# A four-layer attention and experts model on one core: the softmax division's transfers issued by ScalarE, the output bias added by GpSimd, and loads and projection chunks moved within the beginnings of two expert stages

## The chip, the core and the metric

The kernel runs on one core of one Trainium2 chip. A core has four compute engines that take their instructions in order and meet by semaphores: TensorE (PE; its weight loads are listed as PEld), VectorE (DVE), ScalarE (ACT) and GpSimd (POOL), and SyncE (SP), which here only issues DMA transfers. ACT and POOL issue DMA transfers too, as instructions in their own streams. The metric is the time of one execution on the device in microseconds, lower is better.

## The reference

Four layers work on x of shape (4, 512, 256) in float32, each a gated cross attention over a context of 1601 positions and a gated feed-forward stage. The attention of layers 0, 1 and 2 has 16 heads of depth 16:

```python
q = (layernorm(x) @ Wq + bq)   # layer 1 also rotates q and k (rope)
k, v = ctx @ Wk + bk, ctx @ Wv + bv
attn = softmax(q k^T / scale)              # (4, 16, 512, 1601)
x = x + tanh(g) * ((attn @ v) @ Wo + bo)
```

The feed-forward stage of layer 0 is one linear layer with quantised input and ternary weights. Those of layers 1 and 2 are mixtures of 8 experts, of which each row of x takes the one with the highest gate (relu in layer 1, gelu and a capacity in layer 2):

```python
idx = argmax(softmax(x @ gate))            # one expert per row
y[r] = act(x[r] @ w1[idx] + b1[idx]) @ w2[idx] + b2[idx]
```

Layer 3 has an attention with one head of depth 256, and a feed-forward stage that takes two of 8 experts per row.

## The kernel before

**Attention (layers 0, 1 and 2).** The four batches are worked off one after the other, and in each the 16 heads in NG = 4 groups of HG = 4 heads. A group is 13 key tiles of 128 positions times 4 heads, 52 jobs. A job is one matmul of scores s (L1320, on PE) and one exponential e_t (L1412, on ACT). After each key tile PE multiplies e_t with the values of the four heads into pv (L1334). Beside these jobs PE computes maxima of scores for a group some way ahead (m, L1298), which DVE reduces (L1181). `Plan` writes the order of all this down once as a list of units; each engine goes through the whole list and carries out its share, so the place of a unit in the list is its place in each engine's stream. `attend(g, b, *work)` lays the 52 jobs of a group out and spreads other generators of units evenly between them.

**The division by the softmax sums.** When a group's 13 tiles are done, ACT copies pv (outputs and sums of four heads, 128x512) into z (L1419). The rest belongs to the next group: `normalise` gives, one step after the other, the units sum, rec, spread, a step without a unit, and norm.

- sum: SP waits for z and issues rc<-z (L915: the sums, as 128x16) and four ot<-z (L918: the outputs).
- rec: DVE waits for these five transfers (one semaphore, "moved", counts all) and takes the reciprocal of rc (L1204).
- spread: SP waits for the reciprocal, stores rc to DRAM (L927 sums<-rc), waits until that has landed, and loads it back, once for each of 64 partitions (L930 ot<-sums).
- norm: after every second group DVE multiplies the outputs of 8 heads with these reciprocals (L1207).

Then, once for each batch, PE projects with Wo, and DVE adds gate times the product to x and adds the scaled output bias bob (L1213, one per row tile, 16 per layer). The transfers of the division stand in SP's queue among loads and stores of keys and values; between two batches of layer 1 they stand behind the stores of split queries (qready, L94), which wait for GpSimd.

**Other work on ACT.** In a middle group ACT also takes over the values of a finished group for the next batch (v<-vn, L1406, unit take), and in layer 2 it issues beside each take a transfer that clears a part of a table in DRAM (xregion<-zero, L1429, ten times).

**The experts (layers 1 and 2).** The stage normalises x, transposes it (L150), computes the gates (L2382), from them each row's place (L2391, L2392), and scatters the rows to the places by indirect DMA (xs<-xn). SP loads the tiles of rows back (xt<-xs, L2160), and PE runs the two layers of the experts. Into the beginning of layer 1's stage is woven the projection of keys and values of the next attention in chunks of 512 positions (`Prepared`: L322 keys, L330 values on PE, L349 and following on ACT, splits into parts by the engines that its last argument names, stores by SP). In layer 2's stage SP loads the experts' second weights (L2146, eight matrices of 1 MB) and three pieces of the context for the stage after (kT, L1508), and a piece is let out only when a buffer is free of the piece ahead of it.

Of the kernel before, what the change touches and what calls it, by code (L numbers as in the profile page):

```python
# [12 lines left out]
B, T, D, S2 = 4, 512, 256, 1601  # L13
# [422 lines left out]
NORM_STEPS = 5  # L436

MOVES = 1 + HG + 2
# [26 lines left out]
class Plan:  # L465
# [16 lines left out]
    def add(self, kind, **f):  # L482
# [15 lines left out]
        if kind in ("pv", "turn", "sum", "rec", "spread", "norm", "take", "peak"):  # L498
            u.n = self.next(kind)
# [193 lines left out]
def head_attention(kn, w, gate, scale, rope, mask, ready, setup, late):  # L693
# [4 lines left out]
    with ctx:  # L698
# [72 lines left out]
        for name, n in (("s_full", plan.count["s"]), ("s_free", plan.count["s"]), ("m_full", plan.count["m"]),  # L771
# [3 lines left out]
                        ("filled", 2), ("b_scaled", 1), ("bv_made", 1), ("x_done", 1)):  # L775
# [3 lines left out]
        sig("moved", DMA).close(MOVES * NG * B)  # L779
        ends = ["x_done", "s_free", "z_full", "r_full", "td", "moved"]  # L780
# [27 lines left out]
def head_sp(kn, a):  # L808
# [39 lines left out]
    for at, u in enumerate(plan.units):  # L848
# [50 lines left out]


def head_sum_sp(kn, a, u):

    sp, z_full, m_full, moved = kn.nc.sync, kn.sema("z_full"), kn.sema("m_full"), kn.sema("moved", DMA)
    sp.wait_ge(z_full.sem, z_full.at(u.n + 1))
    if u.n:
        sp.wait_ge(moved.sem, moved.at(MOVES * u.n))
    if u.b:
        outs = [x for x in a.plan.units if x.kind == "out" and x.b == u.b - 1]
        sp.wait_ge(m_full.sem, m_full.at(outs[-1].m + 1))
    elif a.p and u.g == 0:  # L910

        for f in range(a.p.RING):
            kept = kn.sema(f"p_k{f}", DMA)
            sp.wait_ge(kept.sem, kept.at(a.p.stores[f]))
    sp.dma_start(a.rc[:], a.z[HD::P // HG, :]).then_inc(moved.sem, DMA)  # L915
    for j in range(HG):
        to, of = HG * HD * (u.g % 2) + HD * j, P // HG * j
        sp.dma_start(a.op[to:to + HD, u.g // 2, :], a.z[of:of + HD, :]).then_inc(moved.sem, DMA)  # L918


def head_spread_sp(kn, a, u):

    sp, r_full, moved = kn.nc.sync, kn.sema("r_full"), kn.sema("moved", DMA)
    sums = kn.dram["sums"]
    sp.wait_ge(r_full.sem, r_full.at(u.n + 1))
    sp.wait_ge(moved.sem, moved.at(MOVES * u.n + 1 + HG))
# [2158 lines left out]
```

## Time and profile before

| what | value |
|---|---|
| time before, median of 3 runs | 3891.18 us (3888.99 to 3891.73) |
| the profiled execution's own time | 3877.86 us |
| span of the profile | 3876.7 us |
| mean granted clock of PE | 0.938 |
| busy share of the span: PE, DVE, ACT, POOL | 88%, 56%, 52%, 17% |
| chain that ended last: PE, DVE, DMA, ACT, SP's queue | 65%, 14%, 7%, 3%, 2% |

The span is that of the instructions in one execution recorded by the hardware profiler; the profiled execution's own time is 1.2 us longer, and both lie 13 us under the median of the runs without a profile. A busy share is an average over stages of different kinds; the rows below come from the stages that the change touches. The attention of layer 0 lies at 0 to 857 us of the span, that of layer 1 at 1042 to 1838, layer 1's experts at 1838 to 2147, layer 2's attention at 2147 to 2920, and its experts from there to about 3150.

### The profile page before, as it was taken

The numbers are of one execution on the slowest core, as the hardware profiler recorded it, in microseconds if no ns is written. First come the engines' busy times: TensorE is split into PE (matmuls) and PEld (weight loads), VectorE is DVE, ScalarE is ACT, GpSimd is POOL, SyncE is SP. The second block draws the span as 40 slices with busy tenths as digits, with TensorE's granted clock in tenths as the row PEclk, the third lists the DMA queues.
The fourth block names the chain that finished last, engine by engine and source line by source line (L and its number), as shares of the span: only waits on it lengthen the run. The fifth ranks groups of instructions, "written<-read, shape, count | busy, mean of one in ns | idle before, by whom it ended". The sixth has DMA issues, their size and how long they took to land.

```text
span 3876.7 us, 52367 instructions
## 1 busy us (share of the span) xinstructions
PE 3409.0 (88%) x18396; PEld 1775.9 (46%) x18396; DVE 2180.8 (56%) x3567; ACT 2033.8 (52%) x4490; POOL 653.1 (17%) x700
## 2 busy tenths in 40 slices
PE   5899999978588899997799699889986979987997
PEld 3333333325332233332588333223325956677996
DVE  6767676736757677873401477768843033265334
ACT  2566666653236566766333167567771322244664
POOL 2111111001125331000302131210002020022331
PEclk8999999999779999999899699999997989998998
DMA  8132323105664343310865555654207521042555
GB/s 191 43 102 63 102 63 102 24 26 185 165 181 118 94 106 74 61 24 14 276 219 176 170 157 119 173 115 100 78 10 277 177 89 56 13 139 88 179 179 177
DMA packets 314686, 456.02 MB, mean 118 GB/s; under 512 B 66315, under 2 KB 234195, under 8 KB 312251
## 3 DMA queue, kind: packets, MB, share of 16 engines
q1 hardware_dynamic: 243382, 292.39, 27.5%
q0 software_dynamic: 29568, 104.65, 7.9%
q10 hardware_dynamic: 41477, 55.63, 5.1%
q8 instruction: 150, 2.46, 0.3%
q14 instruction: 109, 0.89, 0.1%
HBM read 292.46 MB, written 153.91 MB: 115 GB/s over the span
## 4 chain that ended last, share of the span: by engine, by line
PE 65%; DVE 14%; DMA 7%; issue 5%; POOL 4%; ACT 3%; SPq 2%; ACTq 0%; POOLq 0%; DVEq 0%
PE pv L1334 14%; PE m L1298 10%; DVE mxp L1181 10%; PE s L1320 9%; PE h L2794 5%; PE y L2802 5%; PE h L2368 4%; PE y L2377 3%; PE y L1779 2%; PE s L1759 2%; PE s L1265 2%; PE m L1342 1%; ACT e_t L1412 1%; PE s L1282 1%; DMA ot<-sums 1%
## 5 line engine op out<-in xcount | busy, mean ns | idle before, releaser
L1181 DVE TENSOR_REDUCE mxp<-m 128x1 f32<-128x802 f32 x1536 | 1447.7, 985 | 522.4 <-PE m L1298 519.8
L1412 ACT ACTIVATE e_t<-s 128x512 f32<-128x512 f32 (+1 forms) x2496 | 1338.9, 600 | 569.3 <-PE s L1320 568.6
L1298 PE MATMUL m<-kaug,qaug 97*128 97x401 bf16 x3072 | 811.4, 347 | 111.1 <-DVE mxp L1181 60.9
L1320 PE MATMUL s<-qaug,kaug 100*128 100x512 bf16 (+1 forms) x2496 | 857.4, 386 | 22.7 <-ACT e_t L1412 18.4
L1334 PE MATMUL pv<-e_t,v 128*32 128x512 f32 (+1 forms) x4992 | 670.2, 609 | 0.2
L1320 PEld LDWEIGHTS s<-qaug,kaug 100*128 100x128 bf16 (+1 forms) x2496 | 228.1, 99 | 715.6 <-ACT e_t L1412 496.6
L1298 PEld LDWEIGHTS m<-kaug,qaug 97*128 97x128 bf16 x3072 | 273.8, 100 | 521.3 <-DVE mxp L1181 280.5
L127 POOL TENSOR_TENSOR rstd<-rstd,mhalf 128x16 f32<-128x16 f32 (+2 forms) x9 | 24.2, 2687 | 1203.2 <-DVE rstd L120 1203.2
L2864 ACT ACTIVATE ez<-h,b 128x128 f32<-128x128 f32 x440 | 119.8, 387 | 160.0 <-PE h L2794 160.0
L1334 PEld LDWEIGHTS pv<-e_t,v 128*32 128x32 f32 (+1 forms) x4992 | 98.6, 108 | 214.6 <-ACT e_t L1412 155.5
L2255 DVE SCALAR_TENSOR_TENSOR y<-y,b 128x256 f32<-128x256 f32 x39 | 16.6, 424 | 309.5 <-PE y L2377 309.5
L2666 DVE TENSOR_SCALAR ez<-ez 128x1024 f32<-128x1024 f32 x55 | 38.1, 694 | 225.9 <-ACT z L2864 225.9
L1071 POOL TENSOR_TENSOR kr<-kf,ks 128x512 f32<-128x512 f32 (+1 forms) x78 | 77.9, 999 | 497.3 <-ACT ks L1384 493.1
L2451 ACT ACTIVATE hT<-h,b 128x128 f32<-128x128 f32 x312 | 84.7, 382 | 127.6 <-PE h L2368 127.5
L2368 PE MATMUL h<-xtT,w 128*128 128x128 f32 x1248 | 149.8, 280 | 0.4 <-ACT xtT L2468 0.3
L2802 PE MATMUL y<-w,hT 128*128 x624 | 143.0, 383 | 5.7 <-DVE hT L2667 5.7
L2368 PEld LDWEIGHTS h<-xtT,w 128*128 128x128 f32 x1248 | 146.5, 196 | 1.1 <-ACT xtT L2468 1.0
L2794 PE MATMUL h<-xtT,w 128*128 128x128 f32 x1248 | 147.0, 276 | 0.0
L2794 PEld LDWEIGHTS h<-xtT,w 128*128 128x128 f32 x1248 | 143.9, 193 | 0.1
L2377 PE MATMUL y<-w,hT 128*128 x624 | 140.9, 379 | 0.0
L2802 PEld LDWEIGHTS y<-w,hT 128*128 128x128 f32 x624 | 116.7, 192 | 20.9 <-issue 6.3
L2864 ACT ACTIVATE z<-h,b 128x128 f32<-128x128 f32 x440 | 122.5, 453 | 0.0
(370 smaller groups left out, 3560.6 us busy)
## 6 DMA issues: line engine op xcount, KB each, us to landing
w<-in_L_w POOLq DMA_DIRECT2D x78, 1024.0 KB, 5.2
w<-in_L_w SPq DMA_DIRECT2D x24, 1024.0 KB, 12.8
xregion<-zero ACTq DMA_DIRECT2D x10, 2056.0 KB, 12.5
kaug<-kparts SPq DMA_DIRECT2D x16, 1200.8 KB
kaug<-kready SPq DMA_DIRECT2D x32, 600.4 KB
kaug<-kready SPq DMA_DIRECT2D x16, 1200.8 KB
vn<-values SPq DMA_DIRECT2D x8, 1536.0 KB
values<-p_vb ACTq DMA_DIRECT2D x21, 512.0 KB, 4.5
```

Of the source, the lines that this page charges most:

```text
L1071: kn.settle(eng, own, eng.tensor_tensor(rest, src, parts[0], ALU.subtract))
L1181: dve.tensor_reduce(a.mxp[:, u.g % 2, half, n:n + 1], a.m_slot[u.m % 2][:].rearrange("p (a n) -> p a n", a=2)[:, :, 0:PIECE + 1], AX.XY, A ...
L1298: m = pe.matmul(slot[:, 512 * k:512 * k + PIECE + 1], a.qaug[0:R_MAX, u.g, j, P * qc:P * qc + P], a.kaug[0:R_MAX, u.g, j, k0:k0 + PIECE + ...
L1320: pe.matmul(slot[0:KW[u.k], :], a.kaug[0:R_ALL, u.g, u.j, P * u.k:P * u.k + KW[u.k]], a.qaug[0:R_ALL, u.g, u.j, :], start=True, stop=True) ...
L1334: m = pe.matmul(a.pv[32 * j:32 * j + 32, :], a.v[0:KW[u.k], u.k, u.g, VW * j:VW * j + 32], a.e_t[0:KW[u.k], u.n % 2, j, :], start=u.k == 0 ...
L1412: act.activation(a.e_t[0:KW[u.k], e % 2, u.j, :], a.s_slot[u.s % 3][0:KW[u.k], :], ACT.Exp).then_inc(s_free.sem, 1)
L2368: m = pe.matmul(a.h_slot[i % 2][:, P * f:P * f + P], a.w1[:, w1_at, c, P * f:P * f + P], xT(c), start=c == 0, stop=c == DC - 1)
L2377: m = pe.matmul(a.y_slot[i % 2][:, 0:D], a.hT[:, i % 2, f, :], w2(f), start=f == 0, stop=f == FC - 1)
L2451: t = act.activation(a.hT[:, p, f, :], slot[:, P * f:P * f + P], func, bias=bias(f))
L2794: m = pe.matmul(a.h_slot[i % 2][:, P * f:P * f + P], w1[:, c, P * f:P * f + P], xT(c), start=c == 0, stop=c == DC - 1)
L2802: m = pe.matmul(a.y_slot[i % 2][:, 0:D], a.hT[:, i % 2, f, :], w2(f), start=f == 0, stop=f == FC - 1)
L2864: t = act.activation(to[:, p, P * f:P * f + P], slot[:, P * f:P * f + P], func, bias=bias(f))
```

## The change

It has four parts.

1. **The division's transfers are issued by ACT.** `head_sum_sp` and `head_spread_sp` go from SP, and `head_sum_act`, `head_low_act` and `head_spread_act` come to ACT, in the same places of the list of units. A new unit, low, holds the store sums<-rc, which stood in spread before; `normalise` has six steps instead of five. The count is split: "moved" counts the four ot<-z, "summed" the other three transfers, and the reciprocal waits for rc<-z alone.
2. **The output bias is added by GpSimd.** At the unit bias, early in the stage, GpSimd adds bob to x in four instructions per layer (128x1024 each); the 16 additions per layer on DVE go, and the wait for the multiply-add ahead of each.
3. **Layer 1's experts.** The prepared projection's first part of two chunks becomes two parts of one chunk each, both split by GpSimd.
4. **Layer 2's experts.** All eight loads of second weights stand ahead of the second and third piece of the context.

```diff
@@ Plan
-NORM_STEPS = 5
+NORM_STEPS = 6
     def normalise(self, g, b):
-        for kind in ("sum", "rec", "spread"):
+        for kind in ("sum", "rec", "low", "spread"):
             self.add(kind, b=b, g=g)
             yield
...
@@ SP
-        elif u.kind == "sum":
-            head_sum_sp(kn, a, u)
-        elif u.kind == "spread":
-            head_spread_sp(kn, a, u)
...
@@ POOL
+        elif u.kind == "bias":
+            pool.wait_ge(b_made.sem, b_made.at(3))
+            for b in range(B):
+                xb = kn.x[:, TT * b:TT * b + TT, :]
+                pool.tensor_tensor(xb, xb, a.bob[:].rearrange("p (t n) -> p t n", t=1).to_broadcast([P, TT, D]),
+                                   ALU.add).then_inc(biased.sem, 1)
...
@@ DVE
         elif u.kind == "rec":
-            dve.wait_ge(moved.sem, moved.at(MOVES * u.n + 1 + HG))
+            dve.wait_ge(summed.sem, summed.at(3 * u.n + 1))
             dve.reciprocal(a.rc[:], a.rc[:]).then_inc(r_full.sem, 1)
         elif u.kind == "norm":
-            dve.wait_ge(moved.sem, moved.at(MOVES * 2 * (u.n + 1)))
+            dve.wait_ge(moved.sem, moved.at(HG * 2 * (u.n + 1)))
+            dve.wait_ge(summed.sem, summed.at(3 * 2 * (u.n + 1)))
...
         elif u.kind == "out":
+            if u.k == 0:
+                dve.wait_ge(biased.sem, biased.at(u.b + 1))
             dve.wait_ge(m_full.sem, m_full.at(u.m + 1))
             dve.scalar_tensor_tensor(xt, a.m_slot[u.m % 2][:, 0:D], a.gate, xt, ALU.mult, ALU.add).then_inc(m_free.sem, 1)
-            dve.wait_ge(m_free.sem, m_free.at(u.m + 1))
-            i = dve.tensor_tensor(xt, xt, a.bob[:], ALU.add)
...
@@ ACT
+        elif u.kind == "sum":
+            head_sum_act(kn, a, u)
+        elif u.kind == "low":
+            head_low_act(kn, a, u)
+        elif u.kind == "spread":
+            head_spread_act(kn, a, u)
...
+def head_sum_act(kn, a, u):
...
+    act.wait_ge(z_full.sem, z_full.at(u.n + 1))
+    if u.n:
+        act.wait_ge(moved.sem, moved.at(HG * u.n))
+        act.wait_ge(summed.sem, summed.at(3 * u.n))
...
+    act.dma_start(a.rc[:], a.z[HD::P // HG, :]).then_inc(summed.sem, DMA)
+    for j in range(HG):
+        to, of = HG * HD * (u.g % 2) + HD * j, P // HG * j
+        act.dma_start(a.op[to:to + HD, u.g // 2, :], a.z[of:of + HD, :]).then_inc(moved.sem, DMA)
...
+def head_low_act(kn, a, u):
...
+    act.wait_ge(r_full.sem, r_full.at(u.n + 1))
+    act.dma_start(sums.rearrange("j (a c) -> (j a) c", a=P // HG), a.rc[:]).then_inc(summed.sem, DMA)
...
+def head_spread_act(kn, a, u):
...
+    act.wait_ge(summed.sem, summed.at(3 * u.n + 2))
+    lo = HG * HD * (u.g % 2)
+    act.dma_start(a.rs[lo:lo + HG * HD, u.g // 2, :],
+                 kn.dram["sums"].rearrange("j (a n) -> j a n", a=1).to_broadcast([HG, HD, T])).then_inc(summed.sem, DMA)
...
@@ experts
-                           ((2, ("pool",)), (1, ("dve",)), (5, ("dve",)), (4, ("dve",))))
+                           ((1, ("pool",)), (1, ("pool",)), (6, ("dve",)), (4, ("dve",))))
...
-        if a.f and e in (0, NE // 2):
-            fold_context_sp(kn, a.f, 3 if e == 0 else 0)
+        if a.f and e == 0:
+            fold_context_sp(kn, a.f, 3)
         sp.dma_start(a.w2[:, e, :, :], w["w2"][e].rearrange("(f p) n -> p f n", p=P)).then_inc(ld_w.sem, DMA)
...
     if a.f:
-        fold_context_sp(kn, a.f, 1)
+        for b in range(2):
+            fold_context_sp(kn, a.f, b)
```

ACT's stream in a middle group of layer 2, before the change. COPY z is the end of the group ahead, and each ACTIVATE is one exponential; s_178 to s_180 are the three buffers of scores:

```order
L1419 COPY z<-pv 128x512
...
L1412 ACTIVATE e_t<-s_179 128x512
L1429 DMA xregion<-zero 2048x1x257
L1406 COPY v<-vn 128x13x4x16
L1412 ACTIVATE e_t<-s_180 128x512
```

The same group after the change:

```order
L1391 COPY z<-pv 128x512
...
L1410 DMA rc<-z 128x1x16
L1413 DMA ot<-z 16x512 x4
...
L1439 DMA xregion<-zero 2048x1x257
L1371 COPY v<-vn 128x13x4x16
L1377 ACTIVATE e_t<-s_180 128x512
...
L1421 DMA sums<-rc 128x16
...
L1428 DMA ot<-sums 64x1x512
```

Seven transfers now stand between ACT's exponentials: five together some five exponentials after z, the store five exponentials behind the clear and the take, and the load back eight further on.

PE's stream at the beginning of layer 1's experts, before the change. L322 and L330 with p_ctx are the prepared projection of 512 positions, L2382 the gates, and L2391 and L2392 the rows' places; ahead of the rows of L150 stands one more run of chunks:

```order
L150 MATMUL y_147<-ident,hT 128x128 x2
L2382 MATMUL b_142<-gw,xnT 128x8 x32
L322 MATMUL h_144<-p_ctx,p_wk 128x512 x4
L330 MATMUL h_145<-p_wv,p_ctx 128x256 x4
L330 MATMUL h_144<-p_wv,p_ctx 128x256 x4
L2391 MATMUL b_142<-oh,tri 128x128
L2392 MATMUL b_143<-oh,ones 128x128
L322 MATMUL h_145<-p_ctx,p_wk 128x65 x4
L330 MATMUL h_144<-p_wv,p_ctx 65x256 x2
```

The same place after the change:

```order
L150 MATMUL y_147<-ident,hT 128x128 x2
L2394 MATMUL b_142<-gw,xnT 128x8 x32
L322 MATMUL h_145<-p_ctx,p_wk 128x512 x4
L330 MATMUL h_144<-p_wv,p_ctx 128x256 x4
L330 MATMUL h_145<-p_wv,p_ctx 128x256 x4
L2403 MATMUL b_142<-oh,tri 128x128
L2404 MATMUL b_143<-oh,ones 128x128
L322 MATMUL h_144<-p_ctx,p_wk 128x512 x4
L330 MATMUL h_145<-p_wv,p_ctx 128x256 x4
L330 MATMUL h_144<-p_wv,p_ctx 128x256 x4
L322 MATMUL h_145<-p_ctx,p_wk 128x65 x4
L330 MATMUL h_144<-p_wv,p_ctx 65x256 x2
```

Of two chunks that stood ahead of the transposes of L150 one has gone behind the places' matmuls.

SP's queue at the beginning of layer 2's experts, before the change:

```order
L1508 DMA kT<-in_ctxT 128x2x1601
L2146 DMA w_202<-in_L_w 128x8x256 x4
L1508 DMA kT<-in_ctxT 128x2x1601
L2146 DMA w_202<-in_L_w 128x8x256 x4
L1508 DMA kT<-in_ctxT 128x2x1601
L2160 DMA xt<-xs 128x256 x5
```

The same place after the change:

```order
L1518 DMA kT<-in_ctxT 128x2x1601
L2156 DMA w_202<-in_L_w 128x8x256 x8
L1518 DMA kT<-in_ctxT 128x2x1601 x2
L2171 DMA xt<-xs 128x256 x5
```

The second piece of the context now stands behind the last four matrices instead of ahead of them.

## Rows read from the trace of the kernel before

**Rows 1.** windows: busy us of PE, PEld, DVE, ACT, POOL; clock, DMA share, GB/s

```profile
1600.00:1700.00 100.00, 97.05 (x559) 31.43 (x557) 80.79 (x107) 72.32 (x135) 0.00 (x0) 1.00 0.21 41
```

**Rows 2.** DVE's reciprocals, layer 2: start, us, engine, line, op, tiles, idle before

```profile
2511.56 0.24 DVE L1204 RECIPROCAL rc<-rc 128x16 f32<-128x16 f32 x1
...
2550.61 0.24 DVE L1204 RECIPROCAL rc<-rc 128x16 f32<-128x16 f32 x1
...
2807.96 0.24 DVE L1204 RECIPROCAL rc<-rc 128x16 f32<-128x16 f32 x1
...
2846.94 0.24 DVE L1204 RECIPROCAL rc<-rc 128x16 f32<-128x16 f32 x1
```

**Rows 3.** waits: who for whom, us in total, times, longest

```profile
DVE rc L1204 <- DMA ot<-z: 145.5, 11, 29.9
DVE ot L1207 <- DMA ot<-sums: 52.9, 7, 13.8
```

**Rows 4.** the end of layer 2's attention, ACT and DVE in order of time

```profile
2903.08 0.58 ACT L1419 COPY z<-pv 128x512 f32<-128x512 f32 x1 [1.19 <-PE pv L1334]
...
2908.17 0.25 DVE L1204 RECIPROCAL rc<-rc 128x16 f32<-128x16 f32 x1 [29.87 <-DMA ot<-z]
...
2920.15 0.42 DVE L1213 TENSOR_TENSOR x<-x,bob 128x256 f32<-128x256 f32 x1
```

**Rows 5.** DVE's waits ahead of three norms, in order of time

```profile
1350.41 1.00 DVE L1207 TENSOR_TENSOR ot<-ot 128x512 f32<-128x512 f32 x1 [13.80 <-DMA ot<-sums]
...
2432.66 1.37 DVE L1207 TENSOR_TENSOR ot<-ot 128x512 f32<-128x512 f32 x1 [12.59 <-DMA ot<-sums]
...
2608.26 0.69 DVE L1207 TENSOR_TENSOR ot<-ot 128x512 f32<-128x512 f32 x1 [9.48 <-DMA ot<-sums]
```

**Rows 6.** SP's DMA issues in order of time, layer 1, between two batches

```profile
1340.32 1.58 SPq L94 DMA_DIRECT2D qready<-ks  x3
...
1343.87 0.52 SPq L927 DMA_DIRECT2D sums<-rc  x1
1346.78 0.57 SPq L930 DMA_DIRECT2D ot<-sums  x1
```

**Rows 7.** SP's issues of one group's store and load, layer 2, beside a clear

```profile
2511.83 0.34 SPq L927 DMA_DIRECT2D sums<-rc  x1
2520.23 0.59 SPq L930 DMA_DIRECT2D ot<-sums  x1
```

**Rows 8.** SP's DMA issues of one group's sums and parts

```profile
1632.70 0.61 SPq L915 DMA_DIRECT2D rc<-z  x1
1633.35 2.46 SPq L918 DMA_DIRECT2D ot<-z  x4
```

**Rows 9.** ACT in order of time around that clear and a take

```profile
2510.88 0.56 ACTq L1429 DMA_DIRECT2D xregion<-zero  x1
2511.47 0.90 ACT L1406 COPY v<-vn 128x832 f32<-128x832 f32 x1
```

**Rows 10.** DMA issues by kind: KB each, median us from issue to landing

```profile
xregion<-zero ACTq DMA_DIRECT2D x10, 2056.0 KB, 12.5
...
xt<-xs SPq DMA_DIRECT2D x39, 128.0 KB, 3.1
```

**Rows 11.** the beginning of layer 1's experts, PE and ACT in order of time

```profile
1853.62 3.60 PE L322 MATMUL h<-p_ctx,p_wk 128*128 128x512 f32 x8
1857.05 3.62 PE L330 MATMUL h<-p_wv,p_ctx 128*128 128x256 f32 x16
...
1904.32 0.69 ACT L349 ACTIVATE p_kf<-h,p_bk 128x512 f32<-128x512 f32 x1 [12.96 <-DMA kready<-p_ks]
```

**Rows 12.** layer 2's experts' beginning: SP's issues, then the critical chain

```profile
2962.89 15.33 SPq L2146 DMA_DIRECT2D w<-in_L_w  x4
...
2991.30 5.97 DMA xs<-xn,to_u
...
2997.29 7.07 DMA xt<-xs
```

More of the change, by code:

```diff
@@ L497, in add @@
             u.m = self.next("m")
-        if kind in ("pv", "turn", "sum", "rec", "spread", "norm", "take", "peak"):
+        if kind in ("pv", "turn", "sum", "rec", "low", "spread", "norm", "take", "peak"):
             u.n = self.next(kind)
@@ L778, in head_attention @@
             sig(name, DMA).close(n)
-        sig("moved", DMA).close(MOVES * NG * B)
-        ends = ["x_done", "s_free", "z_full", "r_full", "td", "moved"]
+        sig("moved", DMA).close(HG * NG * B)
+        sig("summed", DMA).close(3 * NG * B)
+        ends = ["m_free", "s_free", "z_full", "r_full", "td", "moved", "summed"]
         if not ready:
@@ L898, in head_sp @@
                              a.tm[16 * k:16 * k + 16, :]).then_inc(td.sem, DMA)
[L901 to L926, printed above, removed]
-    sp.dma_start(sums.rearrange("j (a c) -> (j a) c", a=P // HG), a.rc[:]).then_inc(moved.sem, DMA)
-    sp.wait_ge(moved.sem, moved.at(MOVES * u.n + 2 + HG))
-    lo = HG * HD * (u.g % 2)
-    sp.dma_start(a.rs[lo:lo + HG * HD, u.g // 2, :],
-                 sums.rearrange("j (a n) -> j a n", a=1).to_broadcast([HG, HD, T])).then_inc(moved.sem, DMA)
 def head_ready_sp(kn, a, n_of):
@@ L1139, in head_dve @@
     turns = units("turn")
-    ot_full, moved = kn.sema("ot_full"), kn.sema("moved", DMA)
+    ot_full, moved, summed, biased = kn.sema("ot_full"), kn.sema("moved", DMA), kn.sema("summed", DMA), kn.sema("biased")
     ld_q = kn.sema("ld_q", DMA)
@@ L1348, in head_act @@
     s_full, s_free, m_free, pv_done = (kn.sema(n) for n in ("s_full", "s_free", "m_free", "pv_done"))
-    z_full, v_taken, b_scaled, filled = (kn.sema(n) for n in ("z_full", "v_taken", "b_scaled", "filled"))
+    z_full, v_taken, b_made, filled = (kn.sema(n) for n in ("z_full", "v_taken", "b_made", "filled"))
     ld_k = kn.sema("ld_k", DMA)
     rope = a.rope is not None
-    moved = kn.sema("moved", DMA)
+    moved, summed = kn.sema("moved", DMA), kn.sema("summed", DMA)
     if not a.ready:
@@ L1417, in head_act @@
             if n:
-                act.wait_ge(moved.sem, moved.at(MOVES * (n - 1) + 1 + HG))
+                act.wait_ge(moved.sem, moved.at(HG * n))
+                act.wait_ge(summed.sem, summed.at(3 * (n - 1) + 1))
             act.copy(a.z[:], a.pv[:]).then_inc(z_full.sem, 1)
+def head_sum_act(kn, a, u):
+    act, z_full, m_full = kn.nc.scalar, kn.sema("z_full"), kn.sema("m_full")
+    moved, summed = kn.sema("moved", DMA), kn.sema("summed", DMA)
+    act.wait_ge(z_full.sem, z_full.at(u.n + 1))
+    if u.n:
+        act.wait_ge(moved.sem, moved.at(HG * u.n))
+        act.wait_ge(summed.sem, summed.at(3 * u.n))
+    if u.b:
+        outs = [x for x in a.plan.units if x.kind == "out" and x.b == u.b - 1]
+        act.wait_ge(m_full.sem, m_full.at(outs[-1].m + 1))
+    elif a.p and u.g == 0:
+        for f in range(a.p.RING):
+            kept = kn.sema(f"p_k{f}", DMA)
+            act.wait_ge(kept.sem, kept.at(a.p.stores[f]))
+    act.dma_start(a.rc[:], a.z[HD::P // HG, :]).then_inc(summed.sem, DMA)
[3 more added lines that the diff above has]
+def head_low_act(kn, a, u):
+    act, r_full, summed = kn.nc.scalar, kn.sema("r_full"), kn.sema("summed", DMA)
+    sums = kn.dram["sums"]
+    act.wait_ge(r_full.sem, r_full.at(u.n + 1))
+    act.dma_start(sums.rearrange("j (a c) -> (j a) c", a=P // HG), a.rc[:]).then_inc(summed.sem, DMA)
+def head_spread_act(kn, a, u):
+    act, summed = kn.nc.scalar, kn.sema("summed", DMA)
+    act.wait_ge(summed.sem, summed.at(3 * u.n + 2))
+    lo = HG * HD * (u.g % 2)
+    act.dma_start(a.rs[lo:lo + HG * HD, u.g // 2, :],
+                 kn.dram["sums"].rearrange("j (a n) -> j a n", a=1).to_broadcast([HG, HD, T])).then_inc(summed.sem, DMA)
 def clear_act(kn, a, nth):
@@ L2196, in experts_pool @@
     if a.p and a.p.in_parts:
-        prepare_split(kn, a.p, a.p.keys_of(0), pool, "pool")
+        for part in range(2):
+            prepare_split(kn, a.p, a.p.keys_of(part), pool, "pool")
     pool.wait_ge(zeroed.sem, zeroed.at(XTILES))
@@ L2922, in setup_dve @@
     dve, cst = kn.nc.vector, kn.cst
-    ident, ready = kn.sema("ident", DMA), kn.sema("set")
+    ident, ready = kn.sema("tables", DMA), kn.sema("set")
     dve.memset(cst["ones"][:], 1.0)
```

35 lines of the change are left out of this document (14 added, 21 removed).

## The prediction

> **What bounds the kernel now.** I read the busy time by stretch first, then the waits, then single engines in order of time at the places that the change touches. In the middle of an attention stage PE is busy 97.05 of 100 us at a granted clock of 1.00, DVE 80.79 and ACT 72.32 [rows 1]: PE is the bound, and the two others have idle time, but only in small pieces. A group lasts 39.0 us (the distance of two reciprocals, [rows 2]), so a key tile takes 39.0 / 13 = 3.0 us and a job 39.0 / 52 = 0.75 us. ACT is idle 27.68 of 100 us, that is 0.83 us per key tile. What holds ACT for longer than its slack stops PE, which has three buffers of scores and so can be three jobs ahead.
>
> The waits that the change aims at are in the second view. DVE waits 145.5 us for ot<-z ahead of the reciprocal, and 52.9 us for ot<-sums ahead of the norm [rows 3]. The first is almost worthless: three of its 11 waits are about 29.9 us long and stand at the ends of the stages, where DVE has nothing else to do (the last row but one of [rows 4] is one of them). Of the second, 13.80 us are one wait in layer 1 and 12.59 + 9.48 = 22.1 us two in layer 2 [rows 5].
>
> **The change part by part.** *What leaves SP.* In layer 1 the store sums<-rc is issued at 1343.87, right behind stores of split queries that SP could begin only at 1340.32, and the load ot<-sums at 1346.78 [rows 6]; DVE was idle until 1350.41 [rows 5], and this idle time holds up the output projection and the maxima. With the division off SP's queue the wait goes: -13. In layer 2 the two waits lie beside a clear. Behind the clear's issue the store took from 2511.83 to 2520.23 before the load could be issued [rows 7], where in layer 1 it took 1343.87 to 1346.78 [rows 6]. The changed order puts the load of the shorter groups (those that also hold the output) three jobs behind the same clear, or the store five exponentials behind it; such a wait comes back in another place. I take 0, with 22 us of gain as the bound.
>
> *What comes to ACT.* The issues take 0.61 + 2.46 = 3.07 us for the five of a group's sum [rows 8], and I take the same time for ACT: its own issue of a clear takes 0.56 us against 0.34 to 0.61 for single ones on SP [rows 7, 8, 9]. The store and the load back, 0.34 and 0.59 us [rows 7], fit each in one tile's idle 0.83 us and cost nothing; without this cover they cost 0.9 us a group. The five stand in one place. What can hide of 3.07 us? Some 0.5 us lie beneath the exponential that is still running. A clear and a take together, 0.56 + 0.90 = 1.46 us in one place [rows 9], cost nothing: the group with them lasts 39.05 us (2511.56 to 2550.61), one without 38.98 (2807.96 to 2846.94) [rows 2]. So 3.07 - 0.5 - 1.46 = 1.1 us are left. It falls 16 times in each of three stages, less the last group of each, which has no exponentials behind it: 45 x 1.1 = +50. Bounds: if PE's three jobs of lead hide 3 x 0.75 us, 3.07 - 0.5 - 2.25 = 0.3 us and +14 are left; if nothing hides but the running exponential, 2.6 us and +117. I take the value that a row supports, that 1.46 us are free, and not more.
>
> By the Trainium skill, page DMA: Bandwidth & Descriptors, section Issuing engines are not separate DMA queues, transfers started by any engine run on the same 16 DMA engines, and issuing on several of them saves only the sequencer's time. By that rule the transfers land no faster from ACT, and the issue time is merely moved from an engine that has it to spare to one that feeds PE.
>
> *The clears.* Ten clears of 2056 KB each take 12.5 us to land [rows 10]. In eight of these groups the store is now issued some 3.75 us (five jobs) behind the clear, by the same engine, and the load back 13 jobs or 9.75 us behind it. ACT waits there for the store's landing. If the store lands only with the clear, ACT stands 12.5 - 9.75 = 2.8 us, eight times, 22 us. If it lands in the 8.4 us of [rows 7] counted from its issue, 3.75 + 8.4 - 9.75 = 2.4 us. If it lands as quickly as in [rows 6], nothing. Part of a wait is again hidden in ACT's slack; I take half of the 22: +11, bounds 0 and 22.
>
> By the same page, section Queues, rings and completion order, ACT has one row of rings, each ring is worked off in order, and the count of a transfer lands only after every earlier write of its DMA engine. By this rule the upper bound of 22 holds; the trace of before shows a late store behind a clear, 8.4 us, though from another queue.
>
> *Output bias.* 48 additions of 0.42 us [rows 4] leave DVE. 36 of them, 15 us, lie beside PE's work and DVE is not the bound there; one third is taken as seen, since the output's chain PE, DVE, buffer is short: -5 (0 to -15). The additions on GpSimd fall into the beginnings, where x is not needed again before the first output.
>
> *The ends of the three stages.* z is ready at 2903.08 + 0.58 = 2903.66, and the reciprocal ends at 2908.42 [rows 4], when the fifth transfer has landed. Now it waits only for the first, ACT is through its five issues at 2903.66 + 3.07 = 2906.73, and the store follows: -1.7. The last addition of the bias goes too: -0.4. Three stages: -6.
>
> *Layer 1's experts.* Of two chunks ahead of the transposes on PE one goes: 1853.62 to 1860.67, 7 us [rows 11]. Gates, places, scatter and the first tile move ahead by it, and the chunk comes to stand where PE waits for the scatter. ACT stands 12.96 us for a store of the parts at 1904.32 [rows 11], on the same path of the projection; with GpSimd splitting both parts that wait may move, not grow into PE's. -7 (0 to -10).
>
> *Layer 2's experts.* SP needs 15.33 us for the first four matrices' issue [rows 12], and the last four stand behind a piece of context that waits for a buffer. The last scatter is issued at 2991.30 and lands 5.97 us later, the first xt<-xs takes 7.07 us where the median is 3.1 [rows 10, 12]: it shares the DMA engines with those matrices. With them earlier I take 4 us for the load and 2 for the scatter: -6 (-2 to -9).
>
> **Sum.** +50 - 13 + 0 + 11 - 5 - 6 - 7 - 6 = +24. The profiled execution took 3877.86 us, which would become 3902; the median of the runs, 13.3 us above it, becomes 3891.18 + 24 = **3915 us**.
>
> **Rivals.**
> *The hold is hidden* (faster). PE's lead of three jobs covers the five issues: 0.3 us instead of 1.1, so +14 instead of +50: 3915 - 36 = 3879. For it speaks that PE is not held at all by 1.46 us; against it, that PE at 97% has little to catch up with. All other terms sum to -26, so the change breaks even at 26 / 45 = 0.58 us per group; between (26 - 8) / 45 = 0.40 and 34 / 45 = 0.76 us no difference would be seen, as 0.2%, about 8 us, is what a measurement here can tell from none.
> *Late landings.* The small transfers land as late from ACT as they did from SP, beside larger ones: layer 1's wait returns (+13), and each clear costs its whole 2.8 us (+11): 3939. [rows 7] speaks for it, [rows 6], where a queue and not a landing was late, against it.
> *Nothing is hidden.* 2.6 us in each group: +67, 3982. Against it stands the free 1.46 us of [rows 2].
> *The edits cancel*: a hold of 0.40 to 0.76 us, 3883 to 3899.
>
> **How the numbers follow.** The forecast's case (a hold of 0.76 to about 1.6 us, ordinary landings, 3899 to 3938) gets 0.45, late landings 0.12, nothing hidden 0.07, the band between 0.14, the hidden hold 0.22. Slower by over 0.2%: 0.45 + 0.12 + 0.07 = 0.64; within: 0.14; faster: 0.22. The range leaves out the case of nothing hidden and the far side of the hidden hold, with layer 2's 22 us gained as well: 3870 to 3945. The likeliest case alone has 3899 to 3938.
>
> **What would show it.** In the profile after, a middle group should last about 40.1 us instead of 39.0, at the same clock, with a pause of PE ahead of a matmul of scores, released by ACT's exponential, some six jobs behind each z. ACT should show its five issues in 3.1 us. The 13.80 us wait of layer 1 should be gone, the ends of the stages 2 us shorter each. If ACT stands ahead of ot<-sums in layer 2 for 2 to 3 us, the clears cost what I took for them. I am wrong if the groups keep 39.0 us (the three buffers cover all of it), or if an issue on ACT takes clearly less or more than the 0.6 us of SP's.

## The result and the profile after

The changed kernel takes 3977.89 us (median of 4 runs, 3971.58 to 3983.09) against 3891.45 us before (4 runs): +86 us, a ratio of 1.022 (95% interval 1.0204 to 1.0237). I had forecast 3915 us, in 3870 to 3945. It is slower, as forecast, but by three and a half times as much, and close to the rival "nothing is hidden" (3982 us) to which I had given 0.07.

The page of the changed kernel first, then its waits (who for whom, us in total, times, longest):

```profile
span 3970.4 us, 52360 instructions
...
PE 3445.7 (87%) x18396; PEld 1781.3 (45%) x18396; DVE 2162.1 (54%) x3519; ACT 2031.8 (51%) x4490; POOL 681.2 (17%) x712
```

```profile
DVE mxp L1146 <- PE m L1263: 643.0, 622, 30.8
PEld s L1285 <- ACT e_t L1377: 615.2, 728, 3.9
...
DVE rc L1169 <- DMA rc<-z: 144.0, 8, 31.8
...
ACT e_t L1377 <- DMA ot<-z: 79.8, 29, 3.6
...
DVE ot L1173 <- DMA ot<-sums: 46.0, 8, 11.0
```

The busy times of PE, DVE and ACT are those of before within 1.1%: the work is the same. Of the 94 us of longer span 37 are PE's busy time (3445.7 us against 3409.0), as the same matmuls ran longer at a lower clock in some stretches; the rest are pauses. The reciprocal's 145.5 us of waiting [rows 3] are 144.0 us now: they lay at the ends of stages and were worth nothing, as said. A new row has come: ACT stands ahead of an exponential for its own issues of ot<-z (the view names the transfer that was issued, but ACT was busy issuing it), 79.8 us in 29 of the 45 groups.

Below, the time in which ACT issues the five transfers of a group's sum in one go is called the hold. It lasts 3.09 to 3.20 us in 33 of the 45 groups, and PE's pause behind such a hold is mostly 1.6 us, at full clock before and after it. One of these groups, ACT first, then PE:

```profile
1662.89 0.59 ACTq L1410 DMA_DIRECT2D rc<-z  x1
1663.51 2.48 ACTq L1413 DMA_DIRECT2D ot<-z  x4
...
1666.68 0.39 PE L1285 MATMUL s<-qaug,kaug 100*128 100x512 bf16 x1 [1.63 <-ACT e_t L1377]
```

The group ahead of it is one of the dearest: its hold of 4.00 us is the second longest of the 45. In order of time, first ACT, with the issues that answer to [rows 8], then PE:

```profile
1618.51 0.61 ACTq L1410 DMA_DIRECT2D rc<-z  x1
1619.14 3.37 ACTq L1413 DMA_DIRECT2D ot<-z  x4
1622.56 2.07 ACT L1377 ACTIVATE e_t<-s 128x512 f32<-128x512 f32 x4 [3.59 <-DMA ot<-z]
```

```profile
1619.30 0.38 PE L1285 MATMUL s<-qaug,kaug 100*128 100x512 bf16 x1
1619.61 1.07 PE L1299 MATMUL pv<-e_t,v 128*32 128x512 f32 x8
...
1623.21 0.61 PE L1285 MATMUL s<-qaug,kaug 100*128 100x512 bf16 x1 [2.54 <-ACT e_t L1377]
...
1627.04 1.94 PE L1299 MATMUL pv<-e_t,v 128*32 128x512 f32 x8
```

PE fills the three buffers, finishes what it has at 1620.7, and stands 2.54 us until the first exponential behind the hold has freed one. Then come matmuls of nearly double length: pv takes 1.94 us instead of 1.07. The windows of this stretch (busy us of PE, PEld, DVE, ACT and POOL, granted clock, DMA share, GB/s) show why:

```profile
1615.00:1620.00 5.00, 4.91 (x30) 1.62 (x32) 3.86 (x5) 2.96 (x6) 0.00 (x0) 1.00 1.01 167
1620.00:1623.00 3.00, 0.67 (x8) 0.00 (x0) 0.82 (x1) 0.44 (x1) 0.00 (x0) 0.97 0.28 56
1623.00:1626.00 3.00, 2.79 (x8) 1.19 (x9) 1.37 (x2) 2.22 (x5) 0.00 (x0) 0.50 0.05 14
1626.00:1629.00 3.00, 3.00 (x13) 0.45 (x11) 1.77 (x3) 1.08 (x2) 0.00 (x0) 0.50 0.00 0
...
1632.00:1637.00 5.00, 4.92 (x32) 1.57 (x24) 3.76 (x5) 4.06 (x9) 0.00 (x0) 1.00 0.02 2
```

PE was busy 0.67 of the 3 us to 1623, and in the next 6 us its granted clock was 0.50, the lower level of 1.2 GHz, before it was 1.00 again. Not every pause costs clock. In the changed kernel the clock fell, in or behind the pause, in all eleven groups whose longest pause at the hold was 1.9 us or more, for 3.5 to 7.5 us; in 8 of the 28 with 1.57 to 1.81 us, for 3.5 to 4 us; and in none of the six with 1.29 us or less.

The second new wait is in layer 2. ACT around one clear (answering to [rows 7, 9]):

```profile
2568.77 0.65 ACTq L1439 DMA_DIRECT2D xregion<-zero  x1
2569.46 0.90 ACT L1371 COPY v<-vn 128x832 f32<-128x832 f32 x1
2570.26 2.29 ACT L1377 ACTIVATE e_t<-s 128x512 f32<-128x512 f32 x4
2572.25 0.33 ACTq L1421 DMA_DIRECT2D sums<-rc  x1
...
2582.10 0.59 ACTq L1428 DMA_DIRECT2D ot<-sums  x1
2582.73 2.56 ACT L1377 ACTIVATE e_t<-s 128x512 f32<-128x512 f32 x5 [3.76 <-DMA sums<-rc]
```

The load back is issued 9.85 us behind the store and 13.3 us behind the clear, and ACT's exponentials stand 3.76 us for the store's landing. The distances of reciprocals in such groups show both waits together, 44.6 and 47.0 us against 39.05 in [rows 2]:

```profile
2374.30 0.24 DVE L1169 RECIPROCAL rc<-rc 128x16 f32<-128x16 f32 x1
...
2418.90 0.24 DVE L1169 RECIPROCAL rc<-rc 128x16 f32<-128x16 f32 x1
...
2465.94 0.24 DVE L1169 RECIPROCAL rc<-rc 128x16 f32<-128x16 f32 x1
```

The waits of DVE ahead of the norms [rows 5] went in layer 1 only. In layer 2 the two between batches came back, 9.24 and 11.04 us for 12.59 and 9.48:

```profile
1368.99 1.49 DVE L1173 TENSOR_TENSOR ot<-ot 128x512 f32<-128x512 f32 x1
...
2488.24 0.69 DVE L1173 TENSOR_TENSOR ot<-ot 128x512 f32<-128x512 f32 x1 [9.24 <-DMA ot<-sums]
...
2680.68 0.69 DVE L1173 TENSOR_TENSOR ot<-ot 128x512 f32<-128x512 f32 x1 [11.04 <-DMA ot<-sums]
```

Where the time went, by stage. Each stage ends with DVE's last norm of an attention; the columns are distances in the profiled executions, and the last one (from layer 2's last norm to the end) holds layer 2's experts and layer 3. The lower rows are the experiments of the next section.

| kernel | layer 0's attention | to layer 1's last norm | to layer 2's last norm | rest | half clock |
|---|---|---|---|---|---|
| before | 857.6 | 973.5 | 1082.3 | 963.3 | 46 |
| changed | 890.7 | 976.2 | 1144.6 | 958.9 | 74 |
| 1, all seven on SP | 855.7 | 966.0 | 1069.8 | 959.7 | 53 |
| 2, division's part alone | 892.0 | 987.3 | 1129.9 | 964.2 | 73 |
| 4, store and load on SP | 884.3 | 996.5 | 1107.6 | 959.9 | 67 |
| 3, four ot<-z on SP | 852.9 | 943.7 | 1078.5 | 953.8 | 37 |
| 5, two of them on SP | 861.4 | 946.1 | 1091.5 | 961.3 | 38 |
| 6, parts one by one | 852.5 | 949.3 | 1077.3 | 958.1 | 33 |
| 7, changed, late clears | 891.6 | 976.4 | 1086.0 | 960.3 | 54 |
| 8, four on SP, late clears | 850.4 | 940.8 | 1055.0 | 955.7 | 30 |

"Half clock" is the sum of (1 - granted clock) over windows of 2 us in the three attention stages, from the first reciprocal of each to its last norm, in us; two traces of one and the same kernel (experiments 8 and 9) have 30 and 26, so a difference of 4 says nothing. The changed kernel loses 33 us in layer 0, 3 in layer 1 and 62 up to layer 2's last norm, and gains 4 behind it.

### The profile page after: what moved, and what is told of

The parts are those of the page before. It is cut to its first block, busy times and chain, and to the rows that moved or that the text cites. A ratio compares the mean times of both kernels' runs of the same rounds, so it can differ in the third digit from the quotient of the medians.

```text
span 3970.4 us, 52360 instructions
## 1 busy us (share of the span) xinstructions
PE 3445.7 (87%) x18396; PEld 1781.3 (45%) x18396; DVE 2162.1 (54%) x3519; ACT 2031.8 (51%) x4490; POOL 681.2 (17%) x712
## 4 chain that ended last, share of the span: by engine, by line
PE 66%; DVE 11%; DMA 9%; issue 4%; ACT 4%; ACTq 2%; POOL 2%; SPq 1%; another core or an unknown queue 0%; POOLq 0%; DVEq 0%
PE pv L1299 14%; PE m L1263 11%; PE s L1285 10%; DVE mxp L1146 8%; PE h L2806 5%; PE y L2814 5%; PE h L2380 3%; PE y L2389 3%; PE y L1789 2%; PE s L1769 2%; DMA sums<-rc 2%; ACT e_t L1377 2%; PE s L1230 2%; DMA ot<-z 2%; DMA ot<-sums 1%
## 5 line engine op out<-in xcount | busy, mean ns | idle before, releaser
L1285 PE MATMUL s<-qaug,kaug 100*128 100x512 bf16 (+1 forms) x2496 | 875.3, 392 | 112.6 <-ACT e_t L1377 103.6
L1263 PE MATMUL m<-kaug,qaug 97*128 97x401 bf16 x3072 | 820.0, 350 | 93.4 <-DVE mxp L1146 47.4
L1299 PE MATMUL pv<-e_t,v 128*32 128x512 f32 (+1 forms) x4992 | 688.1, 624 | 0.2
## 6 DMA issues: line engine op xcount, KB each, us to landing
w<-in_L_w SPq DMA_DIRECT2D x24, 1024.0 KB, 12.7
xregion<-zero ACTq DMA_DIRECT2D x10, 2056.0 KB, 13.7
```

The source lines that it names most:

```text
L1263: m = pe.matmul(slot[:, 512 * k:512 * k + PIECE + 1], a.qaug[0:R_MAX, u.g, j, P * qc:P * qc + P], a.kaug[0:R_MAX, u.g, j, k0:k0 + PIECE + ...
L1285: pe.matmul(slot[0:KW[u.k], :], a.kaug[0:R_ALL, u.g, u.j, P * u.k:P * u.k + KW[u.k]], a.qaug[0:R_ALL, u.g, u.j, :], start=True, stop=True) ...
L1299: m = pe.matmul(a.pv[32 * j:32 * j + 32, :], a.v[0:KW[u.k], u.k, u.g, VW * j:VW * j + 32], a.e_t[0:KW[u.k], u.n % 2, j, :], start=u.k == 0 ...
```

## The experiments

Time differences are to the kernel before on the same chip, measured beside them (3881.85 us for experiments 1 to 4, 3875.85 for 5 to 8, 3875.30 for 9 to 12), since its time differed by up to 16 us between these measurements; the changed kernel itself stands at +86. "Parts" are the four ot<-z, "store" is sums<-rc and "load" is ot<-sums.

**1. All seven transfers on SP** (the places and the two counts of the change stay). The new functions are the changed kernel's, with the engine as an argument:

```diff
@@ head_act
-        elif u.kind == "sum":
-            head_sum_act(kn, a, u)
-        elif u.kind == "low":
-            head_low_act(kn, a, u)
-        elif u.kind == "spread":
-            head_spread_act(kn, a, u)
@@ head_sp and head_ready_sp
+        elif u.kind == "sum":
+            head_sum_on(kn, a, u, sp, ("rc", "ot"))
+        elif u.kind == "low":
+            head_low_on(kn, a, u, sp)
+        elif u.kind == "spread":
+            head_spread_on(kn, a, u, sp)
```

> The changed kernel with all seven transfers of the division issued by SP again, in the places and with the two counts that the change gave them. Theory of the hold (ACT's issues stop the exponentials, and in layer 2 its wait for the store adds to it): nearly all of the +86 us goes, the other parts of the change stay, 3865 to 3885 us; a middle group without projection lasts 39.0 us again, where the changed kernel has 40.7 or more. Rival, places (the extra step makes the reciprocals come back later, and DVE waits): the time stays over 3940 us. Rival, bias (GpSimd's additions cost what the division does not): over 3900 us with the loss at the beginnings of the stages.

Measured: 3849.39 us, -32 us, ratio 0.992 (0.9899 to 0.9938). The places and the extra step cost nothing, and what is left of the change gains more than I had expected of it. The whole loss, and 32 us beyond it, is in which engine issues.

**2. The division's part alone** (before, with the seven transfers on ACT; bias and expert stages as before):

> The kernel before with the division's part alone: ACT issues the seven transfers; the bias stays on DVE, and the beginnings of both expert stages are those of before. Theory of the hold: 3985 to 3995 us, that is the changed kernel's 3978 and some 10 us for the parts left out (the trace of the changed kernel gives the two expert stages 4 and 5 us, and I allow the bias 0 to 8). Rival, other parts: if bias and expert stages had cost time, it is under 3970 us.

Measured: 3969.60 us, +88 us, ratio 1.0227 (1.0203 to 1.025). By the expectation it should have been some 10 us over the changed kernel's +86, and was 2 over. (The 3969.60 us alone lie at the rival's bound of 3970, but the kernel before was 10 us faster in this measurement too.) The other parts did not cost time (+88 without them), but that they gained the full sum of their terms here isn't seen; see the open point at the end of the next section.

**3. The four parts on SP** (rc<-z, store and load on ACT):

```diff
+        elif u.kind == "sum":       # head_act
+            head_sum_on(kn, a, u, act, ("rc", ))
+        elif u.kind == "sum":       # head_sp, head_ready_sp
+            head_sum_on(kn, a, u, sp, ("ot", ))
```

> The changed kernel with only the four ot<-z of each group issued by SP; rc<-z, the store and the load back stay on ACT. It splits the cost of the issues from that of the clears. Theory of the hold: ACT's single issues of 0.6 us hide, so layer 0's attention returns to before's time (the changed kernel has 33 us more there), and what is left is ACT's wait for the store behind the clears in layer 2, 30 to 40 us: 3895 to 3915 us. Rival, any issue on ACT costs its whole time: three issues of 1.5 us a group are left, 70 us, over 3935 us.

Measured: 3833.69 us, -48 us, ratio 0.9892 (0.9871 to 0.9913). I was right on layer 0, which falls to 852.9 us, and wrong on the rest: 3895 to 3915 had been expected. Single issues on ACT cost nothing at all, and with the hold gone the wait behind the clears is small too, 1.2 to 1.9 us a group instead of 5 (ACT stands 2.97 us for sums<-rc in one of them, where the clear lands in 12.4 us). Layer 1 gains 30 us on before.

**4. Store and load on SP** (the five issues of the sum stay on ACT):

> The changed kernel with the store and the load back issued by SP; the five transfers of the sum stay on ACT. Theory of the hold: layer 0 stays some 30 us over before, layer 2 loses its extra wait of about 5 us in each of eight groups: 3935 to 3950 us, and groups of layer 2 last 41 us instead of 45. Rival, the five issues alone account for layer 2's groups too: no change, 3970 us and over.

Measured: 3947.14 us, +65 us, ratio 1.0167 (1.0146 to 1.0188), as expected. Layer 2's groups last 40.7 us, layer 0 keeps its loss. Against experiment 1 only the five issues differ: 3947.14 - 3849.39 = 98 us (by stage 28.6 + 30.5 + 37.8), which is 2.2 us for each of 45 groups.

**5. Two of the four parts on SP** (three issues together on ACT, 0.58 + 1.21 = 1.8 us):

```diff
+            head_sum_on(kn, a, u, act, ("rc", "ot"), (0, 1))   # parts 0 and 1, head_act
+            head_sum_on(kn, a, u, sp, ("ot", ), (2, 3))        # parts 2 and 3, SP
```

> The changed kernel with the last two of each group's four ot<-z issued by SP, so that three issues, about 1.8 us, stand together on ACT instead of five. It asks how much of a hold is hidden. With all parts on SP the time was 3834 us, with all on ACT 3978. If the hold is hidden up to 1.96 us, as the prediction took from the free clear and take: about 3834 us. If only about 1.1 us are hidden (the five issues of 3.1 us cost 2.0 us a group in layers 0 and 1): 0.7 us a group, 35 us, about 3870 us. If the hold counts in proportion: half way, about 3900 us.

Measured: 3857.43 us, -18 us, ratio 0.9947 (0.993 to 0.9963). That is 30 us over experiment 3, between the first two values of the expectation (3834 and 3870 us). In layers 0 and 1 it is 8.5 + 2.4 us over experiment 3, 0.36 us for each of 30 groups, where four parts cost 37.8 + 32.5 us (the changed kernel against experiment 3), 2.3 us. The cost isn't in proportion: the second two parts cost five times as much as the first two. (Layer 2 takes 13.0 us more than in experiment 3, and 7.5 lie behind the attentions, where the edit does nothing.) ACT and PE at one such place:

```profile
1574.34 0.58 ACTq L1415 DMA_DIRECT2D rc<-z  x1
1574.96 1.21 ACTq L1419 DMA_DIRECT2D ot<-z  x2
1576.21 3.54 ACT L1381 ACTIVATE e_t<-s 128x512 f32<-128x512 f32 x7 [1.41 <-PE s L1289]
```

```profile
1575.44 1.07 PE L1303 MATMUL pv<-e_t,v 128*32 128x512 f32 x8
1576.86 0.39 PE L1289 MATMUL s<-qaug,kaug 100*128 100x512 bf16 x1 [0.35 <-ACT e_t L1381]
```

PE stands 0.35 us instead of 2.54, and goes on at full clock (the matmul of scores takes 0.39 us, not 0.61). The two kernels agree on what is hidden: a hold of 3.10 us leaves a pause of 1.63, one of 1.82 us a pause of 0.35, so 1.47 us are hidden both times.

**6. The parts one by one** (all seven on ACT, each part in a step of its own; ten steps instead of six):

```diff
-NORM_STEPS = 6
+NORM_STEPS = 10
-        for kind in ("sum", "rec", "low", "spread"):
+        for j, kind in enumerate(("sum", "rec", "low", "spread")):
             self.add(kind, b=b, g=g)
             yield
+            self.add("part", b=b, g=g, k=j)
+            yield
```

> The changed kernel with ACT issuing all seven transfers, but the four ot<-z one at a time, each in a step of its own between the other units (ten steps instead of six). ACT's issue time is the same, 3.9 us a group, and nothing of it stands in one place. Theory of the place (what is hidden depends on how long ACT is held at once): layer 0's attention returns to before's time, and only the clears' wait stays: 3835 to 3860 us. Rival, total issue time counts since ACT is short of time: 3950 us and over.

Measured: 3837.48 us, -38 us, ratio 0.9903 (0.9885 to 0.9921), as expected. ACT issues as much as in the changed kernel, and the groups last 39.0 us. In layers 0 and 1, where there are no clears, this is worth 38 and 27 us. The ten steps also let the load back come later, 12.4 to 12.9 us behind the clear, so part of layer 2's 67 us is the wait behind the clears and not the hold. It is the hold in one piece that costs, not ACT's issue time.

**7. The changed kernel with late clears**, and **8. experiment 3 with late clears**. ACT issues each clear right behind the next load:

```diff
             if a.clears and u.b:
-                clear_act(kn, a, (u.b - 1) * NG + u.g)
+                a.due.append((u.b - 1) * NG + u.g)
...
         elif u.kind == "spread":
             head_spread_act(kn, a, u)
+            while a.due:
+                clear_act(kn, a, a.due.pop(0))
```

> The changed kernel with each clear of layer 2 issued by ACT right behind the load back instead of ahead of the take, so that neither the store nor the load stands behind 2 MB. Nothing else moves. If the store's landing behind the clear is what layer 2 lost beyond the five issues: the load follows the store by 5.9 us again instead of 10.3, groups last 41 us instead of 45, and the time falls by 25 to 36 us, to about 3945 us. Rival, the clears' own traffic slows other loads wherever they stand: no gain, 3970 us and over.

> Both edits: the four ot<-z on SP, and the clears behind the load back on ACT. With the parts on SP alone the time was 3834 us, and the groups of layer 2 with a clear lasted 40.6 us against 39.0. If the store behind the clear is the cause: 8 x 1.6 = 13 us less, about 3821 us, with 39.0 us in these groups. Rival: within 5 us of 3834.

Measured: 3911.51 us, +36 us, ratio 1.008 (1.0059 to 1.010), and 3806.93 us, -69 us, ratio 0.9825 (0.9809 to 0.9842). Both gain more than expected, 50 us (86 to 36) and 21 us in the medians: 59 us of span up to layer 2's last norm in the first (1144.6 to 1086.0), and 24 in the second (1078.5 to 1055.0). Of the first, 36 lie in the eight groups with a clear ahead of the store, 17 between the batches, where the load itself stood behind a clear (the distances 57.3 and 59.9 us become 48.5 and 51.5), and 5 elsewhere in the stage. ACT in experiment 7; the load follows the store by 5.9 us, and the clear follows the load:

```profile
2543.35 0.33 ACTq L1424 DMA_DIRECT2D sums<-rc  x1
...
2549.28 0.59 ACTq L1431 DMA_DIRECT2D ot<-sums  x1
2549.90 0.62 ACTq L1442 DMA_DIRECT2D xregion<-zero  x1
```

**9. Experiment 8 once more**, **10. the same with the bias on DVE**, **11. experiment 6 with late clears**, and **12. experiment 1 with late clears**:

> The version with the four ot<-z on SP, the other three transfers on ACT and the clears behind the load back, once more, as the measure for the three others of this call: a ratio of about 0.982 to the kernel before.

> That version with the output bias on DVE, as in the kernel before. The prediction had 5 us of gain for the bias on GpSimd beside PE's work and 0.4 us at each stage's end. If that is so, this is 5 to 8 us slower than the version beside it (ratio 0.984). Rival: the additions on DVE cost nothing, since DVE has time: within 2 us. Rival: GpSimd's additions, 2.4 us each, cost at the beginnings: this is faster.

> All seven transfers on ACT, one in a place, and the clears behind the load back. With the clears ahead of the store this had a ratio of 0.990, and groups with a clear lasted 39.0 us all the same, since the longer steps leave the store time to land. Theory: only the groups between two batches of layer 2 gain (60.2 and 60.1 us, against 49.7 and 50.9 with the load ahead of the clear), 20 us: ratio 0.985. Rival: no gain, 0.990.

> All seven transfers on SP, and the clears on ACT at the place behind the load back. It tells what the three transfers on ACT are worth once the clears are out of the way. With the clears ahead this had 3849 us. If the waits in layer 2 between batches come from the clears, 10 us are gained there; layer 1's wait behind the query stores in SP's queue (67.7 us for the group between batches against 48.2 with the store on ACT) stays: ratio 0.989 against 0.982. Rival: SP is as good as ACT once the clears are late, 0.984.

Measured: 3807.68 us (-68, ratio 0.9819, 0.9801 to 0.9836); 3818.87 us (-56, 0.9852, 0.9835 to 0.987); 3854.82 us (-20, 0.9937, 0.992 to 0.9953); 3841.09 us (-34, 0.991, 0.9893 to 0.9926). The repeat of experiment 8 agrees within 2 us. The bias on GpSimd is worth 11 us, the upper half of its range and more than the 5 to 8 expected. With all seven on SP the late clears are worth 2 us (-34 against -32), where 10 had been expected. The three single transfers on ACT are worth 33 us (experiment 12 against 9), 16 of it in layer 1 (961.4 against 945.7 us), whose wait stays with SP. Experiment 11 went against its expectation: it is 18 us slower than experiment 6, each against the kernel before, and 16 of them lie in layer 2 (1093.7 against 1077.3 us). In its order one part is issued 2 us behind the clear, and there the issue itself takes longer than the usual 0.54 us: 2.1 to 2.5 us in nine of the ten places, and 8.42 us in the tenth, between two batches (ACT, layer 2):

```profile
2317.59 2.17 ACTq L1386 DMA_DIRECT2D ot<-z  x1
...
2397.27 0.59 ACTq L1438 DMA_DIRECT2D ot<-sums  x1
2397.89 0.65 ACTq L1449 DMA_DIRECT2D xregion<-zero  x1
...
2399.97 8.42 ACTq L1386 DMA_DIRECT2D ot<-z  x1
2408.44 2.06 ACT L1380 ACTIVATE e_t<-s 128x512 f32<-128x512 f32 x4 [7.88 <-issue]
```

Two of the groups with an issue of 2.2 to 2.5 us last 46.3 and 45.1 us instead of 39.0. In each PE stands for a load of queries that SP issued behind the clear, and then runs at the lower clock for 7 to 10 us. The first of them, PE and then a window of the same kind as above:

```profile
2330.26 0.39 PE L1287 MATMUL s<-qaug,kaug 100*128 100x512 bf16 x1 [1.91 <-DMA qaug<-tm]
...
2332.00:2335.00 3.00, 3.00 (x13) 0.92 (x15) 2.37 (x3) 1.65 (x3) 0.00 (x0) 0.50 1.04 225
```

In no other kernel of this study does PE stand for this load in layer 2. So in this order the rival of experiment 7's expectation holds, that the clears' own traffic slows other loads: moving the clears takes a wait from one transfer and may give it to another.

## Why the prediction was wrong

The sign and the mechanism were right: ACT's five issues in one place stop the exponentials, PE runs out of buffers, and the store behind the clear adds to it in layer 2. Two costs were too small, by 48 us each; three gains were larger than forecast and took back a third of that.

- **The hold** (+50, measured +98 by experiments 1 and 4). The step that failed is "3.07 - 0.5 - 1.46 = 1.1 us". The issues took the time that was taken for them, 3.1 us. But the step takes the exponential that is still running off twice. The clear and take that cost nothing also came behind a running exponential; their free 1.46 us already contain it. 3.07 - 1.46 = 1.6 us is what the plain groups show: 39.0 us with all on SP, 40.6 with the five issues on ACT (experiment 4; two of its reciprocals in layer 1 stand below), where 40.1 had been forecast. PE's pauses say the same, with 1.47 us hidden behind holds of 3.10 and of 1.82 us (experiment 5). 45 x 1.6 = 72. Of the 26 us beyond, about 6 are longer holds: nine of the 45 in experiment 4 took 3.3 to 4.2 us, and all together take 145.8 us instead of 45 x 3.10. About 14 go with the clock: over the three stages the half clock sum is 67 us with the five issues and 53 without (an estimate, as two traces of one kernel differ by 4). The last 6 are not separated, and why some issues take longer no run here tells.

```profile
1269.82 0.24 DVE L1177 RECIPROCAL rc<-rc 128x16 f32<-128x16 f32 x1
...
1310.45 0.24 DVE L1177 RECIPROCAL rc<-rc 128x16 f32<-128x16 f32 x1
```

- **The clears** (+11, measured +59 in the spans and 50 in the medians by experiment 7). The step that failed is the half. I took half of 2.8 us for eight groups, because the store might land at its usual speed. It landed with the clear: the load was issued 9.7 to 10.8 us behind the store and 13 to 14 us behind the clear, whose median was 13.7 us here instead of 12.5. In each of these groups the load was issued 0.2 to 0.4 us behind the clear's landing. Its turn on ACT comes 5.9 us behind the store and 9.4 behind the clear, as forecast. So the wait is 3.8 to 4.9 us in each of eight groups, and all of it is seen: 36. The same rule held for the load between two batches, which I had called 0: that is another 17. The pauses also cost clock: layer 2's half clock sum is 40 us in the changed kernel and 15 with late clears. The Trainium skill, page DMA: Bandwidth & Descriptors, section Queues, rings and completion order, has the rule that I had weighed: a completion count lands only after all earlier writes of its DMA engine. The trace agrees with it: the load that waits for the store's count is issued 13.3 us behind a clear that lands in 13.1 us, and 5.9 us behind the store when no clear is ahead. Before the change the same store, issued by SP 1.0 us behind the clear, was in earlier: the load followed 9.4 us behind a clear that landed in 12.4 us [rows 7, 9].
- **Layer 2's removed waits** (0, with 22 as the bound). They would have gone: with store and load on ACT and the clears out of the way layer 2 up to its last norm takes 22 us less than with store and load on SP (1086.0 against 1107.6). In the changed kernel the clears take it back.
- **Layer 1's wait** (-13, measured -20: 996.5 against 976.2 us with store and load on SP and on ACT; 22 between experiments 1 and 3 and 16 between 12 and 9). The place was right; the wait held up more than its own 13.8 us.
- **Output bias** (-5, measured -11, experiments 9 and 10). Of this 9.5 lie in layer 1, 8 of them in one distance between two batches (48.2 against 56.2 us); that it is the output's chain which became shorter is not shown.
- **The ends of the stages** (-6, measured about -4). From z to the last norm layer 2 takes 9.2 us instead of 10.3, 1.1 less and not 1.7, since the store follows at once but the norm still comes 3.8 us behind the load's issue; the last addition's 0.4 us went. ACT and DVE at the end of layer 2's attention, changed kernel, answering to [rows 4]:

```profile
3002.26 0.59 ACT L1391 COPY z<-pv 128x512 f32<-128x512 f32 x1 [1.18 <-PE pv L1299]
...
3004.82 0.25 DVE L1169 RECIPROCAL rc<-rc 128x16 f32<-128x16 f32 x1 [31.80 <-DMA rc<-z]
3006.02 0.59 ACTq L1421 DMA_DIRECT2D sums<-rc  x1
3007.71 0.59 ACTq L1428 DMA_DIRECT2D ot<-sums  x1
3011.46 0.69 DVE L1173 TENSOR_TENSOR ot<-ot 128x512 f32<-128x512 f32 x1 [6.39 <-DMA ot<-sums]
```

- **The expert stages** (-7 and -6, measured -3 and -6, with 2 us given back behind them). From the first to the last statistics of x, layer 1's takes 293.4 us instead of 296.5 and layer 2's 223.3 instead of 229.5; experiment 2, without these edits, has 300.6 and 229.2. In layer 1's the chunk did go from ahead of the transposes, but behind the places' matmuls the chain runs over the splits' stores, 6.66 and 8.34 us, where before it ran over three of 6.04 to 7.31: they got no shorter. The load of the first tile of layer 2's takes 4.64 us instead of 7.07 [rows 12], in the critical chain of the changed kernel:

```profile
3092.55 4.64 DMA xt<-xs
```

The sum of the measured terms is 98 + 59 - 22 - 20 - 11 - 4 - 7 = +93, against +86 in the runs and +94 in the spans. The terms come from different pairs of kernels, so that they add up so well is partly luck.

**The rivals.** "Nothing is hidden" came nearest with its number, and by the wrong way: 1.46 us are hidden in each plain group, and experiment 3 shows that a single issue costs nothing. "The hold is hidden" is out: PE's lead does not cover three jobs' time, as PE has filled the buffers 1.2 us after ACT's issues began (its last matmul of scores ends at 1619.68) and stops after one more pv. "Late landings" was right behind the clears and wrong in layer 1.

**Open.** Experiment 2 should have been slower than the changed kernel by the 18 us that bias and experts gain, and was slower by 2. It is slower in layer 1 (987.3 against 976.2 us) and behind layer 2's last norm (964.2 against 958.9), and faster in layer 2's attention: 821 us from the last statistics of x in layer 1's experts to layer 2's last norm against 844. The clears landed in 12.0 us (median) there and in 13.7 in the changed kernel, and the load followed the store by 8.4 to 9.1 us instead of 9.7 to 10.8. Why the same 2 MB take 1.7 us more in one program than in another no run here tells; of the fourteen traces of this study nine have 12.0 to 12.7 and five 13.0 to 13.7, and one kernel traced twice has 13.0 and 12.5. It wasn't tried with the buffers or the tables moved.

## What to carry to other kernels

An issue on a compute engine costs what the engine's partner can't buffer, so what counts is how long the issues stand in one place: seven issues a group were free one at a time and cost 2.2 us with five together. When a free instruction is used as the measure of slack, everything that hid it is in that measure already, and may not be taken off once more. Small transfers that someone waits for should not stand behind a large one of the same engine; here moving ten clears behind the load was worth 21 to 50 us with the store on ACT. It was worth 2 us with all seven transfers on SP, and cost 18 with the parts issued one by one, where one of them came to stand right behind the clear. With the parts on SP, the rest on ACT and late clears the kernel is at 0.982 of before, faster than both.

## What the runs showed of the hardware

- A pause of 2.54 us of a PE that had been busy 4.91 of 5 us was followed by about 6 us at the lower clock (0.50 in two windows of 3 us), in which matmuls took up to 1.8 times their time; a pause of 0.35 us was not. In the changed kernel the lower clock came with all eleven pauses of 1.9 us or more at a hold, with 8 of the 28 of 1.57 to 1.81 us, and with none of the six shorter ones. Nothing here tells which of the 28 pay.
- The issue of a 32 KB transfer on ACT mostly takes 0.5 to 0.6 us. When it comes 2 us behind the issue of a 2 MB transfer of the same engine it took 2.1 to 2.5 us in nine of ten places and 8.42 us in one; 2.9 us behind such an issue (experiment 6) it took 0.52 to 0.55 us. The 8 KB store issued 3.5 us behind the same clear took 0.33 us to issue and landed with the clear instead.
